# Cross attention and ternary FFN on one core: the product with V' two pairs back, next to the scores, and every transpose of a slot in its middle

## The reference

```python
xn   = layernorm(x)
q, k, v = xn @ Wq, ctx @ Wk, ctx @ Wv          # 16 heads of 64
dots = q k^T * 64**-0.5, causal
x    = x + softmax(dots) v @ Wo + bo
y    = layernorm(x)
aq   = lambda t: round(t * 127/max|t|) / (127/max|t|)    # each row, 8 bits
wq   = lambda w: clip(round(w / mean|w|), -1, 1) * mean|w|
x    = x + aq(silu(aq(y) @ wq(w_gate).T) * (aq(y) @ wq(w_up).T)) @ wq(w_down).T     # 512 hidden
```

## Time and profile before

| | before |
|---|---|
| median of three runs | 822.65 us |
| the profiled execution | 821.9 us, of which 820.1 us from the first to the last instruction |
| TensorE busy | 783.2 us, 96% |
| VectorE busy | 678.8 us, 83% |
| ScalarE busy | 678.9 us, 83% |
| GpSimd busy | 407.3 us, 50% |
| DMA | 20.5 MB, mean 25 GB/s |
| chain that ended last | TensorE 81% of the span, VectorE 8%, "issue" 5%, ScalarE 4% |

### The profile page before, as it was taken

How to read it: one execution, slowest core, us unless ns; L and a number is a source line. 1 busy time by engine, 2 the same in 40 slices (tenths; PEclk the granted TensorE clock), 3 DMA queues, 4 the chain that set the end, 5 groups by cost and what they waited for, 6 DMA issues and landing times.

```text
span 820.1 us, 17819 instructions
## 1 busy us (share of the span) xinstructions
PE 783.2 (96%) x5487; PEld 542.6 (66%) x5550; DVE 678.8 (83%) x1845; ACT 678.9 (83%) x1202; POOL 407.3 (50%) x404
## 2 busy tenths in 40 slices
PE   7899999999999999999999999999999999999983
PEld 5667666766766766676666676676676667666552
DVE  7749888888878887988888888788888888878894
ACT  4688888888888887988888888788888888888882
POOL 1235555454554545555545545555454554544551
PEclk9999999999999999999999999999999999999997
DMA  7100010100101000010100101010010100000000
GB/s 225 53 1 1 15 38 16 39 2 14 40 14 39 13 18 22 13 39 13 38 2 13 39 13 38 14 39 0 13 39 14 39 13 13 1 14 15 1 14 14
DMA packets 37109, 20.50 MB, mean 25 GB/s; under 512 B 1460, under 2 KB 36534, under 8 KB 37046
## 3 DMA queue, kind: packets, MB, share of 16 engines
q1 hardware_dynamic: 37046, 19.84, 8.3%
HBM read 15.64 MB, written 4.19 MB: 24 GB/s over the span
## 4 chain that ended last, share of the span: by engine, by line
PE 81%; DVE 8%; issue 5%; ACT 4%; POOL 1%; DMA 0%; DVEq 0%; POOLq 0%; ACTq 0%
PE ps_s L431 13%; PE ps_a L500 12%; PE ps_s L402 5%; PE ps_s L322 4%; PE ps_kv L402 3%; PE ps_kv L322 3%; PE ps_s L324 3%; PE ps_kv L323 3%; PE ps_s L323 3%; PE ps_s L404 3%; PE ps_b L459 3%; PE ps_s L403 3%; PE ps_a L459 3%; PE ps_kv L403 3%; PE ps_kv L324 3%
## 5 line engine op out<-in xcount | busy, mean ns | idle before, releaser
L872 POOL TENSOR_TENSOR prob<-prob,row_max 128x1024 f32<-128x1024 f32 x64 | 122.0, 1906 | 189.4 <-DVE row_max L747 189.4
L520 ACT ACTIVATE vp<-ps_s 64x512 f32<-64x512 f32 x256 | 151.2, 590 | 33.2 <-PE ps_s L404 28.9
L890 POOL TENSOR_TENSOR prob<-prob,row_rec 128x512 f32<-128x512 f32 x128 | 130.9, 1044 | 56.3 <-DVE row_rec L822 56.3
L520 ACT ACTIVATE vp<-ps_kv 64x512 f32<-64x512 f32 x256 | 151.5, 592 | 5.4
L882 POOL TENSOR_TENSOR hid_b<-hid_q,neg_round 128x512 bf16<-128x512 f32 x64 | 66.7, 1041 | 128.1 <-DVE hid_q L791 128.1
L500 PE MATMUL ps_a<-vp,prob_t 128*64 128x128 f32 x2048 | 125.9, 276 | 1.3 <-DVE x L769 1.2
L431 PE MATMUL ps_s<-kp,xn_t 128*64 128x512 f32 x512 | 124.0, 605 | 2.9 <-ACT vp L520 1.9
L500 PEld LDWEIGHTS ps_a<-vp,prob_t 128*64 128x64 f32 x2048 | 110.6, 137 | 24.4 <-issue 16.3
L744 DVE TENSOR_TENSOR prob<-ps_s,bias_sb 128x1024 f32<-128x1024 f32 x64 | 78.3, 1223 | 54.3 <-PE ps_s L431 53.7
L520 ACT ACTIVATE kp<-ps_s 128x512 f32<-128x512 f32 x130 | 77.8, 599 | 11.9 <-PE ps_s L290 8.2
L849 POOL TENSOR_TENSOR rs<-ve,neg_half 128x1 f32<-128x1 f32 x128 | 70.4, 550 | 33.1 <-DVE ve L669 24.5
(11 more groups left out here) (175 smaller groups left out, 1725.5 us busy)
## 6 DMA issues: line engine op xcount, KB each, us to landing
x_in<-in_x SPq DMA_DIRECT2D x16, 256.0 KB, 2.9
ctx_in<-in_ctx SPq DMA_DIRECT2D x16, 256.0 KB, 3.4
x_res<-in_x SPq DMA_DIRECT2D x16, 256.0 KB, 2.8
out<-x SPq DMA_DIRECT2D x15, 256.0 KB, 2.4
kp<-in_L_xattn_Wk SPq DMA_DIRECT2D x1, 512.0 KB, 4.0
kp<-in_L_xattn_Wq SPq DMA_DIRECT2D x1, 512.0 KB, 4.9
kp<-in_L_xattn_Wv SPq DMA_DIRECT2D x1, 512.0 KB, 6.1
kp<-in_L_xattn_Wo SPq DMA_DIRECT2D x1, 512.0 KB, 6.1
```

The lines of the kernel that those rows point to most:

```text
L520: copy = lambda dst, src, **kw: nc.scalar.activation(dst, src, ACT.Copy, **kw)
L872: p.tensor_tensor(prob[c % 2][:], prob[c % 2][:], rows(row_max[c % 2]), ALU.subtract).then_inc(shifted, 1)
L890: p.tensor_tensor(prob[c % 2][:, heads, :], prob[c % 2][:, heads, :], rows(row_rec[c % 2])[:, heads, :], ALU.mult).then_inc(normed, 1)
```

## The change

On TensorE the product with V' (then of pair s-2, no longer s-1) stands at the head of the slot, directly before the scores of pair s. After the scores come V', K', V', K'; then all transposes (xq, hidden activations, both halves of the probabilities) back to back; then a V' unit, gate, up and down together, two K' units and the last V' unit. The transposes of x move from the end of the group's last slot to its second slot (`x_turn`), one group later, between K' and the last V'. The banks are dealt anew (`V_BANK`, `K_BANK`): the hidden transposes go to ps_g, down goes to ps_b. So gate waits for the copy of the hidden activations, and down for both copies of the probabilities.

ScalarE takes its copies in the new order. VectorE starts its slot with x1 and its statistics (pair s-2), then adds the bias, goes through the FFN input, then the row maximum, then x2 and the hidden rows. GpSimd follows that order. The arithmetic and the number of instructions in a slot are the same.

```diff
-        ps_h = ps_b[:, 0:F // 2].bitcast(BF16)
+        ps_h = ps_g[:, 0:F // 2].bitcast(BF16)
...
-        def v_bank(it, c, u):
-            return (2, 0, 0, 2)[u] if group_ahead(it, c, 1) else (2, 0, 1, 3)[u]
+        def x_turn(it, c):
+            return c % GP == 1 and live(it, c) and group_ahead(it, c, 1) and (not isinstance(it, int) or 2 * it + c // GP > 0)
+        V_BANK, K_BANK = (2, 0, 3, 2), (3, 1, 0, 1)
...
+                makes_k = live(it, c) and group_ahead(it, c, 1)
...
                     if live(it, c):
+                        v_dst = banks[V_BANK[u]]
                         if first(it, c):
                             pe.wait_ge(n_lo_done, u + 1)
                         if u == 0 and live(it, c, 1):
                             pe.wait_ge(v_evac, 8 * s)
                         elif u == 1:
                             pe.wait_ge(biased, s + 1)
-                        elif u and group_ahead(it, c, 1):
-                            pe.wait_ge(v_evac, 8 * s + (4, 2)[u == 3])
+                        elif u == 2 and makes_k:
+                            pe.wait_ge(k_evac, 16 + 4 * s + 1)
+                        elif u == 3:
+                            pe.wait_ge(v_evac, 8 * s + 2)
                         h2, half = u // 2, u % 2
                         hi, lo = (w[:, h2, 4 * half:4 * half + 4, :].rearrange("p a e -> p (a e)") for w in (n_hi, n_lo))
...
-                    k_dst = banks[3] if u in (0, 3) else banks[1]
-                    if live(it, c) and group_ahead(it, c, 1):
+                    if makes_k:
                         if first(it, c) and u == 0:
                             pe.wait_ge(tern_evac, 3)
-                        if u != 1:
-                            pe.wait_ge(k_evac, 16 + 4 * s + (0, None, 2, 1)[u])
-                        k_unit(4 * q + u, 1 - par, k_dst)
+                        if u == 2:
+                            pe.wait_ge(v_evac, 8 * s + 4)
+                        elif u == 3:
+                            pe.wait_ge(k_evac, 16 + 4 * s + 2)
+                        k_unit(4 * q + u, 1 - par, banks[K_BANK[u]])
+                if live(it, c, 2):
+                    pe.wait_ge(pt_evac, 2 * s - 2)
+                    pe.wait_ge(v_evac, 8 * s - 8)
+                    if x_turn(it, c - 1):
+                        pe.wait_ge(xnt_evac, g + 2)
+                    for a in range(HP):
+                        for b in range(2):
+                            t = mm(ps_a[b * S:(b + 1) * S, 0:D], prob_t[:, a, b * S:(b + 1) * S],
+                                   vp[c % 2][:, b, a, :], start=(a == 0), stop=(a == HP - 1))
+                    t.then_inc(attn_ready, 1)
                 if live(it, c):
                     if q == 0:
...
                         if not isinstance(it, int) or group_ahead(it, c - 1, 1):
-                            pe.wait_ge(k_evac, 16 + 4 * s - 1)
+                            pe.wait_ge(k_evac, 16 + 4 * s)
+                        else:
+                            pe.wait_ge(v_evac, 8 * s - 4)
                     for half in range(2):
                         for b in range(2):
...
                     rest_of_setup()
-                early = q == 0 and group_ahead(it, c, 1)
-                if early:
-                    v_quarter(0)
+                v_quarter(0)
+                if makes_k and q == 0:
+                    pe.wait_ge(ctlo_ready, g + 2)
+                k_quarter(0)
+                v_quarter(1)
+                k_quarter(1)
                 if live(it, c, 2):
-                    if live(it, c, 3):
-                        pe.wait_ge(h_step, H_STEPS * (s - 3) + 2)
                     pe.wait_ge(xq_ready, s - 1)
                     nc.tensor.transpose(ps_x, xq[:], id_sb[:]).then_inc(xqt_ready, 1)
-                if live(it, c) and q == 0 and group_ahead(it, c, 1):
-                    pe.wait_ge(ctlo_ready, g + 2)
-                    pe.wait_ge(xnt_evac, g + 2)
                 if live(it, c, 3):
                     pe.wait_ge(hb_ready, s - 2)
...
                     if live(it, c, 2):
                         pe.wait_ge(x1_done, s - 1)
                     prob_transposes(0, ps_a)
+                    pe.wait_ge(normed, 2 * s)
+                    if live(it, c, 4):
+                        pe.wait_ge(x2_done, s - 3)
+                    prob_transposes(1, ps_b)
+                v_quarter(2)
+                if live(it, c, 3):
...
                     pe.wait_ge(xqt_evac, s - 1)
                     mm(ps_g[:, :], xq_t[:], wg_t[:], start=True, stop=True).then_inc(gate_ready, 1)
                     mm(ps_u[:, :], xq_t[:], wu_t[:], start=True, stop=True).then_inc(up_ready, 1)
-                if not early:
-                    v_quarter(0)
-                if live(it, c, 1):
-                    pe.wait_ge(normed, 2 * s)
-                    if live(it, c, 3):
-                        pe.wait_ge(ht_evac, s - 2)
-                    prob_transposes(1, ps_b)
-                k_quarter(0)
                 if live(it, c, 3):
-                    pe.wait_ge(ht_evac, s - 2)
                     if live(it, c, 1):
-                        pe.wait_ge(pt_evac, 2 * s - 1)
+                        pe.wait_ge(pt_evac, 2 * s)
                     for k in range(FB):
-                        t = mm(ps_a[:, D:2 * D], hid_t[:, k, :], wd_t[:, k, :], start=(k == 0), stop=(k == FB - 1))
+                        t = mm(ps_b[:, 0:D], hid_t[:, k, :], wd_t[:, k, :], start=(k == 0), stop=(k == FB - 1))
                     t.then_inc(down_ready, 1)
-                v_quarter(1)
-                k_quarter(1)
-                if live(it, c, 1):
-                    pe.wait_ge(pt_evac, 2 * s)
-                    pe.wait_ge(v_evac, 8 * s)
+                k_quarter(2)
+                k_quarter(3)
+                if x_turn(it, c):
+                    pe.wait_ge(xn_ready, GP * g + 2 * GP)
+                    pe.wait_ge(pt_evac, 2 * s - 1)
+                    transpose_x(1 - par)
+                v_quarter(3)
+                if live(it, c) and q == GP - 1 and group_ahead(it, c, 2):
+                    pe.wait_ge(ctx_loaded[par], 16 * (it + 2))
                     if live(it, c, 3):
                         pe.wait_ge(x2_done, s - 2)
-                    for a in range(HP):
-                        for b in range(2):
-                            t = mm(ps_a[b * S:(b + 1) * S, 0:D], prob_t[:, a, b * S:(b + 1) * S],
-                                   vp[(c - 1) % 2][:, b, a, :], start=(a == 0), stop=(a == HP - 1))
-                    t.then_inc(attn_ready, 1)
-                v_quarter(2)
-                k_quarter(2)
-                k_quarter(3)
-                v_quarter(3)
-                if live(it, c) and q == GP - 1 and group_ahead(it, c, 2):
-                    pe.wait_ge(ctx_loaded[par], 16 * (it + 2))
-                    pe.wait_ge(xn_ready, GP * g + 3 * GP)
-                    pe.wait_ge(x1_done, s)
                     transpose_ctx(par, ps_b)
-                    transpose_x(par)
-            slots(pe, slot, 4 - 1)
+            slots(pe, slot, 3)
         @block.scalar
...
-                                 banks[v_bank(it, c, u)][b * S:(b + 1) * S, :]).then_inc(v_evac, 1)
+                                 banks[V_BANK[u]][b * S:(b + 1) * S, :]).then_inc(v_evac, 1)
...
-                        take_k(1 - par, 4 * q + u, 16 + 4 * s + u + 1, (3, 1, 1, 3)[u])
+                        take_k(1 - par, 4 * q + u, 16 + 4 * s + u + 1, K_BANK[u])
...
+                take_v(0)
+                take_k_quarter(0)
+                take_v(1)
+                take_k_quarter(1)
                 if live(it, c, 2):
                     act.wait_ge(xqt_ready, s - 1)
                     copy(xq_t[:], ps_x, bias=-ROUND).then_inc(xqt_evac, 1)
...
                     copy(flat(hid_t[:, :, :]), ps_h[:, :]).then_inc(ht_evac, 1)
                 take_probs(0, ps_a)
+                take_probs(1, ps_b)
                 if live(it, c, 2):
                     act.wait_ge(gate_ready, s - 1)
                     act.wait_ge(ln2_step, LN2_STEPS * (s - 1))
                     nc.scalar.activation(tanh_sb[:], ps_g[:, :], ACT.Tanh,
                                          scale=g_half[:, (c - 2) % 4:(c - 2) % 4 + 1]).then_inc(tanh_done, 1)
-                if group_ahead(it, c, 1):
-                    take_v(0)
-                    take_probs(1, ps_b)
-                else:
-                    take_probs(1, ps_b)
-                    take_v(0)
-                take_k_quarter(0)
-                take_v(1)
+                take_v(2)
                 if live(it, c) and not first(it, c):
                     exponential(s, c)
-                take_k_quarter(1)
-                take_v(2)
                 take_k_quarter(2)
                 take_k_quarter(3)
+                if x_turn(it, c):
+                    take_x(1 - par, g + 1)
                 take_v(3)
                 if live(it, c) and q == GP - 1 and group_ahead(it, c, 2):
```

(40 more changed lines are left out.)

127 lines of the change are left out of this document (45 added, 82 removed).

## The result

| | before | changed |
|---|---|---|
| median | 822.41 us (820.27 to 823.04, 4 runs) | **948.29 us** (944.64 to 949.50, 4 runs) |
| ratio | | **1.153**, 95% interval 1.149 to 1.157 |
| span of the profiled execution | 820.1 us | 942.8 us |

A forecast was written before the change was run, and what follows sets the result against it. TensorE's queue bounded the kernel before; in the new order TensorE would wait for ScalarE's chain of copies. Groups +72, loop edges +6, last group +6, tail +3 and first four slots +1 sum to +88: 910 us, range 875 to 932.

The forecast's parts named there:

- Edges of the 64-column stretch, -0.20 a slot: On TensorE, two fewer edges between 128-column and 64-column weights, about 0.1 us each, save 0.20 us a slot.
- ScalarE's first copy at 4.78 and the end of the second prob_t at 10.04: Us after the product with V' starts: first V' unit's copy starts at 4.78, probabilities' second half is copied by 10.04.
- The ledger's 12.7: Step-by-step layout of one plain slot across the engines: 12.7 us, against 11.67 before.
- VectorE has just no part in it, and no room: VectorE's 10.62 us of steps end at 16.7, just when the next bias add is due, so it adds no time.
- Group sum 53.1: Four slots, 12.8 + 14.5 + 12.7 + 13.1 = 53.1 us against 47.9; fourteen groups give +72.
- x wait, q = 1 slots 14.5: At q = 1 the product with V' waits for ScalarE's copy of x from ps_a: slot 14.5 us.
- Loop edges +6: Five hardware-loop turns: VectorE's late bias add makes the slot 15.1 us, before 13.23; +6 us in all.
- Rival B: Slower: TensorE also late at loop turns, +13 (923 us); VectorE's ring longer by 0.5, another +28 (938); chance 0.08.
- Last group +6 and tail +3: Three slots without K' copies, 11.8 us instead of 9.77, +6; tail, pair 63's product a slot later, +3.
- A: Faster: the waits are covered and TensorE stays the limit, a slot 11.47, 805 us; chance 0.05.
- C: Slower by half: ScalarE's chain costs only x wait and loop edges, TensorE at 11.9; near 865 us; chance 0.07.
- D: No difference: savings and waits cancel, 822 us; chance 0.03.

The follow-up runs named there:

- the detours repaired: Changed kernel with VectorE's program written out, hid_q and xn2 kept clear of GpSimd, x taken earlier, first slot's row maximum ahead of N's low parts: 871.72 us.
- the version written out: Changed kernel with VectorE's program written out for all slots instead of a hardware loop, other engines keeping theirs: 919.46 us.

## Why the prediction was right in direction and wrong in size

It had the direction and the chain of copies right. Two steps failed: the term for the loop edges, +6, where the runs showed +19.7, and the statement that VectorE has no part in the ring.

- **Edges of the 64-column stretch, -0.20 a slot: right.** 1.80 from product to scores, where 1.90 was the step.
- **ScalarE's first copy at 4.78 and the end of the second prob_t at 10.04: right**, 4.61 and 10.27, or 9.80 with the detours repaired. With the detours repaired a plain slot takes 12.33 against 11.67 before. Of these 0.66 us, 0.27 are shown to be the wait for the second copy, for a run without it gave them back; that the rest is the same chain is argued. The ledger's 12.7 was 0.35 too long.
- **"VectorE has just no part in it, and no room": wrong, and the main mechanism missed.** hid_q took 1.26 us where the 10.62 of the ledger held it at 0.48. It delayed x1, the bias add and the second V' unit in three of four slots (at q = 2 the wait for x hid it); keeping it and xn2 clear of GpSimd gave 18 us. The prediction priced moved instructions at their old durations and did not ask what would run beside them.
- **Group sum 53.1: near, by two errors that cancel.** Outside the loop's effects a group took 12.88 + 14.82 + 12.36 + 13.19 = 53.25, or 52.4 without contention: the ledger too long, contention missing. The term +72 measured +75 (745.4 in the version written out against 670.5 in the kernel before written out).
- **x wait, q = 1 slots 14.5: right** (14.8; 14.4 without contention). Putting x earlier gave 1.4 a group alone and 1.7 with the other repairs.
- **Loop edges +6: mis-sized, the step that failed the number.** Written out against not, 770.75 - 745.40 = 25.35 in the changed kernel and 676.22 - 670.53 = 5.69 in the kernel before: **+19.7**. 13.2 of it stand in the five edge slots, 6.5 in the other slots of the body. The prediction had an edge slot at 15.1: it took 15.60 where the clock held, and 16.30 to 17.75 where TensorE fell to half clock, which the sum had no term for. Rival B came near the number (+13) by another mechanism: it had TensorE's own turn late, and with only VectorE's loop written out the edges are gone. Its second half, a ring of VectorE longer than the ledger's slot, is what the runs show, at 0.2 a slot and not 0.5.
- **First four slots +1: wrong, +7.8**, of which 6.4 in slot 0. The moved row maximum was not followed through N's low parts and wd_t.
- **Last group +6 and tail +3: +9.3 and +11.2.** Longer idling brought the half clock, which the kernel before showed only in its tail. For the last group that is shown by the added matmuls; for the tail it is argued from its 0.73 against 0.82.

The misses add up: 2.9 + 13.7 + 6.8 + 3.3 + 8.2 = 35, from +88 to +122.7. The median lies another 3.7 us above the profiled execution, where the prediction allowed 0.75 (and left that out of its 910: 821.9 + 88 + 0.75 is 910.7). That the group sum came out near is luck, for its two errors cancel. A, C and D fell with the waits that they denied.

## What to carry to other kernels

When an order changes, ask of each moved instruction what the neighbour engines run beside it then: a duration from the old trace holds only with its old company. A kernel bound by TensorE hides loop turns, contention and start-up order in the others' slack; a change that ties the engines into a ring pays for all of them at once, and an idle TensorE then pays again by its clock. Look for such hidden costs first: writing out VectorE's loop alone made the kernel before 0.7% faster.

## What was not expected of the hardware

- A 128x512 float32 tensor_scalar on VectorE took 481 ns alone and 1204 to 1259 ns beside a GpSimd tensor_tensor; a 128x128 one 394 to 404 on the mean in the changed kernel and its repaired form, and 703 and 964 on the mean in the two runs that brought it beside GpSimd's normalization. The bias add from PSUM kept its 1.23 us beside GpSimd.
- VectorE's turn of the hardware loop left up to 2.5 us without an instruction (12.3 over five turns). Written out, these gaps are gone.
- TensorE's granted clock fell from 1.00 to 0.50 after it had been busy 0.42 us of 4.00 in the first slot, and in the last slots around idle stretches of 2.5 us; 48 matmuls with no reader made the kernel 5 us faster.
